# An attention kernel on one core: the first part's sums in the same steps as its scores, V and q/k jobs moved to other steps, and the low parts of the weights taken from SBUF

## What is computed

```
xf = x.reshape(b, c, n)                                # 8, 128, 1024
q = einsum('oc,bcn->bon', Wq, xf) + bq                 # 64 x 1024 for each image
k = einsum('oc,bcn->bon', Wk, xf) + bk                 # 64 x 1024
v = einsum('oc,bcn->bon', Wv, xf) + bv                 # 128 x 1024
attn = softmax(einsum('bci,bcj->bij', q, k), axis=-1)  # 1024 x 1024
out = einsum('bcn,bmn->bcm', v, attn)
return gamma * out + x
```

## Time and profile before

| | us |
|---|---|
| median of 3 runs | 240.18 |
| lowest, highest | 240.05, 241.45 |
| the profiled execution's own time | 239.82 |
| its span in the profile | 238.0 |
| TensorE busy (matmul) in the span | 221.8 (93%) |
| ScalarE busy | 177.9 (75%) |
| GpSimd busy | 177.5 (75%) |
| VectorE busy | 161.0 (68%) |

### The profile page before, as it was taken

The page is one execution under the profiler, slowest core; times in us unless marked ns, Lnnn a source line. Parts: engine busy times, 40 slices in busy tenths (PEclk is TensorE's granted clock), DMA queues, the critical chain, the costliest instruction groups (busy, mean ns, idle before and its releaser), DMA issues.

```text
span 238.0 us, 5352 instructions
## 1 busy us (share of the span) xinstructions
PE 221.8 (93%) x1864; PEld 205.0 (86%) x1864; DVE 161.0 (68%) x345; ACT 177.9 (75%) x342; POOL 177.5 (75%) x162
## 2 busy tenths in 40 slices
PE   6786958799999999999999999999999999999994
PEld 5464857599998999899998999899998999999994
DVE  1676556787776677777776677767776687676334
ACT  2486856668887798778877798778877788778980
POOL 8667665967877788778887787778886866886871
PEclk9999999999999999999999999999999999999999
DMA  3652640067700945048600964039400862100111
GB/s 95 212 211 64 156 136 1 4 144 166 223 0 3 234 120 178 2 106 208 214 10 0 218 153 164 2 89 221 139 0 0 196 159 88 49 0 3 44 48 44
DMA packets 17882, 24.43 MB, mean 103 GB/s; under 512 B 9920, under 2 KB 10688, under 8 KB 17856
## 3 DMA queue, kind: packets, MB, share of 16 engines
q1 hardware_dynamic: 17552, 23.96, 38.6%
q10 hardware_dynamic: 304, 0.13, 0.2%
HBM read 8.59 MB, written 4.19 MB: 54 GB/s over the span
## 4 chain that ended last, share of the span: by engine, by line
PE 80%; DVE 6%; ACT 4%; DMA 3%; issue 3%; POOL 2%; SPq 1%; ACTq 0%; POOLq 0%
PE sums L615 22%; PE sums L629 12%; PE scores L594 11%; PE scores L595 11%; PE work L550 10%; PE work L544 6%; ACT qk_hi L746 2%; DVE qk_lo L840 2%; DMA k_hione<-qk_hi 2%; DMA w_qk<-in_L_conv_Wk 1%; PE work L537 1%; PE work L539 1%; PE work L538 1%; PE sums L550 1%; DVE neg_max L849 1%
## 5 line engine op out<-in xcount | busy, mean ns | idle before, releaser
L476 POOL TENSOR_TENSOR weight_lo<-weight,weight_hi 128x512 bf16<-128x512 f32 x96 | 123.1, 1290 | 40.7 <-ACT weight_hi L788 40.6
L849 DVE TENSOR_REDUCE neg_max<-work 128x1 f32<-128x512 f32 x120 | 82.0, 686 | 12.2 <-PE work L550 12.2
L615 PEld LDWEIGHTS sums<-values,weight_hi 128*128 128x128 f32 x504 | 76.6, 189 | 6.7 <-issue 2.0
L615 PE MATMUL sums<-values,weight_hi 128*128 128x258 f32 x504 | 80.8, 282 | 1.7 <-DVE weight_lo L887 1.7
L788 ACT ACTIVATE weight_hi<-scores 128x512 fp32r<-128x512 f32 x128 | 76.4, 597 | 0.0
L594 PE MATMUL scores<-q_hihi,k_hilo 128*128 128x256 f32 x256 | 71.0, 300 | 0.5 <-ACT weight_hi L788 0.5
L595 PE MATMUL scores<-q_lomax,k_hione 128*128 128x256 f32 x256 | 66.2, 281 | 0.0
L785 ACT ACTIVATE weight<-scores 128x512 f32<-128x512 f32 x96 | 57.5, 599 | 10.0 <-PE scores L595 3.6
L550 PE MATMUL work<-k_hilo,q_hihi 128*128 128x512 f32 x120 | 48.4, 406 | 4.7 <-DVE qk_lo L840 3.3
L594 PEld LDWEIGHTS scores<-q_hihi,k_hilo 128*128 128x128 f32 x256 | 48.3, 189 | 2.1 <-issue 1.6
L595 PEld LDWEIGHTS scores<-q_lomax,k_hione 128*128 128x128 f32 x256 | 48.5, 189 | 1.0 <-issue 0.5
(11 more groups left out here) (85 smaller groups left out, 162.4 us busy)
## 6 DMA issues: line engine op xcount, KB each, us to landing
x_turned_sb<-in_x_turned SPq DMA_DIRECT2D x8, 512.0 KB, 4.6
out<-y_sb SPq DMA_DIRECT2D x15, 256.0 KB, 3.4
x_sb<-in_x SPq DMA_DIRECT2D x7, 512.0 KB, 4.5
q_hihi<-qk_hi SPq DMA_DIRECT2D x12, 256.0 KB, 4.4
q_lomax<-qk_lo SPq DMA_DIRECT2D x7, 256.0 KB, 5.7
k_hione<-qk_hi SPq DMA_DIRECT2D x7, 256.0 KB, 5.2
k_hilo<-qk_hi SPq DMA_DIRECT2D x6, 256.0 KB, 3.2
k_hilo<-qk_lo SPq DMA_DIRECT2D x6, 256.0 KB, 5.1
```

Of the source, the lines that this page charges most:

```text
L476: pool.tensor_tensor(weight_lo[:, r], weight[:, r], weight_hi[:, r], ALU.subtract).then_inc(weight_lo_pool_done, 1)
L615: last = pe.matmul(sums[:, u % 2 * PAIR + it, 0:VCOLS], weight_hi[:, r, part_tile(kt, it)], values[p][:, key_tile(s, kt)], start=(j == 0 a ...
L849: dve.reduce_max(neg_max[:, t, h:h + 1], place, AX.X, negate=True).then_inc(neg_max_done, 1)
```

## The change

The high sums of part 0 are made in steps 0 to 3, in the same steps as the scores two ahead, instead of two steps later; steps 4 and 5 have no high sums, and from step 6 on all is as before. The low sums of part 0 stay in step 5. For this `project_v(0, 1)` goes to the third bank of `sums`, and q and k of image 1 go to the fourth and then the third. VectorE takes the first maximum of chunk 1 ahead of the low part of V. y of part 0 is made at step 6 instead of 8.

"v" jobs for image b + 1 move from k = 11 and 15 to 3 and 15 (7 and 15 for b = 0); "qk" jobs for image b + 2 from k = 6 and 10 to 7 and 11 (10 and 13 for b = 0). The high and low parts of x, the bf16 copies of V and the adding of the bias move with them. `EARLY_MAXES` and two of the "mt" jobs change steps.

VectorE's low parts read `weight` and `weight_hi` from SBUF; ScalarE writes all exact weights to SBUF. Both waits for the shared bank go. The low part of step 2 goes to GpSimd (31 steps on VectorE, 97 on GpSimd).

```diff
 EARLY_MAXES = {0: (1, 1, 1), 1: (1, 2, 1), 2: (1, 3, 1), 3: (1, 4, 1), 4: (1, 5, 1), 5: (1, 6, 1), 6: (1, 7, 1),
-               7: (2, 0, 2), 8: (2, 2, 2), 9: (2, 4, 1), 10: (2, 5, 1), 11: (2, 6, 2),
-               12: (3, 0, 2), 13: (3, 2, 1), 14: (3, 3, 1), 15: (3, 4, 2), 16: (3, 6, 1), 17: (3, 7, 1)}
-MAX_TURNS = {0: ("mt", 0, 1), 3: ("mt", 1, 0), 7: ("mt", 1, 1)}
+               7: (2, 0, 1), 8: (2, 1, 2), 9: (2, 3, 2), 10: (2, 5, 1), 11: (2, 6, 2),
+               12: (3, 0, 1), 13: (3, 1, 1), 14: (3, 2, 2), 15: (3, 4, 1), 16: (3, 5, 2), 17: (3, 7, 1)}
+MAX_TURNS = {0: ("mt", 0, 1), 4: ("mt", 1, 0), 8: ("mt", 1, 1)}
+QK_STEPS, FIRST_QK_STEPS = (7, 11), (10, 13)
+V_STEPS, FIRST_V_STEPS = (3, 15), (7, 15)
+X_HI_STEPS, X_LO_STEPS = (4, 8), (5, 9)
...
-    if k in (6, 10) and b + 2 < BATCHES:
-        jobs.append(("qk", b + 2, (6, 10).index(k)))
-    if k in (11, 15) and b + 1 < BATCHES:
-        jobs.append(("v", b + 1, (11, 15).index(k)))
+    qk_steps, v_steps = (FIRST_QK_STEPS, FIRST_V_STEPS) if b == 0 else (QK_STEPS, V_STEPS)
+    if k in qk_steps and b + 2 < BATCHES:
+        jobs.append(("qk", b + 2, qk_steps.index(k)))
+    if k in v_steps and b + 1 < BATCHES:
+        jobs.append(("v", b + 1, v_steps.index(k)))
...
 def low_on_dve(s):
-    return s % PART_STEPS == DVE_LOW
+    return s >= PART_STEPS and s % PART_STEPS == DVE_LOW
...
 def finish_step(part):
-    return PART_STEPS * part + PART_STEPS + AHEAD + (2 if part == 0 else 0)
+    return PART_STEPS * part + PART_STEPS + AHEAD
...
-                if k in (0, 12) and s > 0 and b + k // 12 < BATCHES:
-                    short_values(b + k // 12, 1 - k // 12)
-                if s in (4, 8):
-                    add_bias((4, 8).index(s))
-                if b == 0 and k in (5, 9) or b > 0 and k in (1, 5) and b + 2 < BATCHES:
-                    rest_of_x(b + 2, (5, 9).index(k) if b == 0 else (1, 5).index(k))
-                if b == 0 and k in (10, 13) or b > 0 and k in (9, 13) and b + 1 < BATCHES:
-                    add_bias(2 * (b + 1) + k // 13)
+                if k == 0 and b > 0:
+                    short_values(b, 1)
+                if k == (10 if b == 0 else 6) and b + 1 < BATCHES:
+                    short_values(b + 1, 0)
+                if s == 4:
+                    add_bias(0)
+                if k == (8 if b == 0 else 1):
+                    add_bias(HALVES * b + 1)
+                if k in X_LO_STEPS and b + 2 < BATCHES:
+                    rest_of_x(b + 2, X_LO_STEPS.index(k))
+                if k == 13 and b + 1 < BATCHES:
+                    add_bias(HALVES * (b + 1))
...
                 if j == 0:
                     wait(pe, y_done, PAIR * (u - 1))
-                    pe.wait_ge(weight_lo_done, low_count(s + DVE_LOW))
...
-            pe.wait_ge(neg_max_done, CHUNK_TILES + 1)
-            project_v(0, 1, sums[:, 0])
+            pe.wait_ge(neg_max_done, CHUNK_TILES + PAIR + 1)
+            project_v(0, 1, sums[:, PAIR])
...
-                if LAG <= s < ALL_STEPS:
-                    if s == LAG:
-                        pe.wait_ge(first_v_rest_done, 1)
+                if s < PART_STEPS:
+                    if s == 0:
                         pe.wait_ge(neg_max_done, CHUNK_TILES + PAIR)
-                    if s == LAG + PART_STEPS:
+                    sums_hi(s)
+                elif PART_STEPS + LAG <= s < ALL_STEPS:
+                    if s == PART_STEPS + LAG:
                         pe.wait_ge(qk_lo_done, HALVES)
                     sums_hi(s - LAG)
-                    if (s - LAG) % PART_STEPS == PART_STEPS - 1:
-                        sums_lo(s - LAG)
-                if s in (1, 2):
-                    pe.wait_ge(neg_max_done, CHUNK_TILES + PAIR + s)
-                    project_qk(1, s - 1, sums[:, PAIR + s - 1])
+                if LAG <= s < ALL_STEPS and (s - LAG) % PART_STEPS == PART_STEPS - 1:
+                    sums_lo(s - LAG)
+                if s == 1:
+                    pe.wait_ge(neg_max_done, MAXES)
+                    project_qk(1, 0, sums[:, PAIR + 1])
+                if s == 2:
+                    pe.wait_ge(first_v_rest_done, 1)
+                    project_qk(1, 1, sums[:, PAIR])
...
-                if low_on_dve(s):
-                    u = s // PART_STEPS
-                    wait(act, y_done, PAIR * (u - 1))
-                    if u == 0:
-                        act.wait_ge(neg_max_done, CHUNK_TILES + PAIR)
-                    if u == 1:
-                        act.wait_ge(qk_lo_done, HALVES)
-                act.activation(exact_weights(s) if low_on_dve(s) else weight[:, r], scores[:, s % 2], ACT.Exp)
+                act.activation(weight[:, r], scores[:, s % 2], ACT.Exp)
...
-                if b == 0 and k in (4, 8) or b > 0 and k in (0, 4) and b + 2 < BATCHES:
-                    round_x(b + 2, (4, 8).index(k) if b == 0 else (0, 4).index(k))
+                if k in X_HI_STEPS and b + 2 < BATCHES:
+                    round_x(b + 2, X_HI_STEPS.index(k))
...
-                dve.tensor_tensor(weight_lo[:, r], exact_weights(s), weight_hi[:, r], ALU.subtract).then_inc(weight_lo_done, 1)
+                dve.tensor_tensor(weight_lo[:, r], weight[:, r], weight_hi[:, r], ALU.subtract).then_inc(weight_lo_done, 1)
...
-            dve.wait_ge(v_hi_done, HALVES)
-            dve.tensor_tensor(values[0][:, quarter(1), 0:CHANNELS], by_tiles(sums[:, 0]),
-                              values[0][:, quarter(1), CHANNELS:2 * CHANNELS], ALU.subtract).then_inc(first_v_rest_done, 1)
             for name, c, i in FIRST_MAXES:
                 do_max(c, i)
+            dve.wait_ge(v_hi_done, HALVES)
+            dve.tensor_tensor(values[0][:, quarter(1), 0:CHANNELS], by_tiles(sums[:, PAIR]),
+                              values[0][:, quarter(1), CHANNELS:2 * CHANNELS], ALU.subtract).then_inc(first_v_rest_done, 1)
```

More of the change, by code:

```diff
@@ L283, in part_banks @@
             return slice(u % 2 * PAIR, (u % 2 + 1) * PAIR)
-        def exact_weights(s):
-            return sums[:, s // PART_STEPS % 2 * PAIR + 1]
         def key_tile(s, kt):
@@ L817, in _ @@
             first_q(1, bank(0))
-            round_v(0, 1, sums[:, 0])
+            round_v(0, 1, sums[:, PAIR])
             exponentials(1)
@@ L825, in _ @@
                 if s in (1, 2):
-                    round_qk(1, s - 1, sums[:, PAIR + s - 1])
+                    round_qk(1, s - 1, sums[:, PAIR + 2 - s])
                 if s >= LAG and (s - LAG) % PART_STEPS == PART_STEPS - 1:
@@ L968, in _ @@
                 if s in (1, 2):
-                    rest_of_qk(1, s - 1, sums[:, PAIR + s - 1])
+                    rest_of_qk(1, s - 1, sums[:, PAIR + 2 - s])
                 if s + 1 < ALL_STEPS and low_on_dve(s + 1):
```

## The result

The changed kernel takes 233.06 us (median of 4 runs, 232.45 to 233.38) against 240.12 (4 runs, 239.71 to 241.45): a ratio of 0.969, 95% interval 0.965 to 0.974. The forecast was 233.2. The profiled execution took 232.45 us with a span of 230.7, 7.4 less than before's profiled one.

The account below looks back on a forecast made before the run. TensorE was taken to set the pace. Early gain 5.1 plus steady gain 2.3 minus 0.4 for VectorE's low parts makes 7.0 us: 239.82 to 232.8, plus 0.36 for the median, 233.2 us; range 231.0 to 236.4.

Parts of the forecast that it names:

- The early steps: Steps 0 to 17, worked out one by one from unit times: step 18 starts at 52.2 us, before 57.31.
- Steps 7 to 12: TensorE's early steps with V and q/k jobs and chunk 2's maxima: from 28.0 us to 40.5 us.
- a job's bank is free 1.7 us after its end: Sums bank of a V or q/k job: free once ScalarE and VectorE have read it, 1.7 us after the job.
- Step 1: Early step with a q/k job of image 1: maximum waits for VectorE's second reduction until 18.76, step ends 20.4 us.
- step 3: Early step on TensorE without a side job: 1.20 us long, ending at 23.7 us.
- The row of maxima: Chunk 2's row, needed by step 14's scores: last maximum 38.6, DMAs 40.05, row 44.05; step 14 gives back 0.8 us.
- The early gain, 5.1: Start to step 18: step 17 ends at 52.2 us where before it was 57.31, so 5.1 us less.
- The steady gain, 2.3: Images after the early steps: V's wait for q/k's bank goes, 0.65 - 0.2 = 0.45 us for each of five images.
- The 0.2 behind k = 11: Steady state: a maximum two steps behind the q/k job at k = 11 just misses its bank, costing about 0.2 us.
- VectorE's low parts: Both inputs in SBUF: 0.69 us alone, up to 1.97 if taking turns with GpSimd; 0.4 us cost over the run.
- 1.3 us of lateness is swallowed: Maximum behind a late low part: its bank is wanted 2.4 us later and reading takes 1.1, so 1.3 us is harmless.
- the wait in step 2: TensorE's 1.66 us idle in step 2, waiting for VectorE's low part in the shared bank: forecast to go.

Follow-up runs that it names:

- e10: Changed kernel with image 2's q/k in steps 11 and 13, chunk 2's last maximum first in step 11, chunk 3's maxima paired in 13 and 15: 231.5 us, 0.964.
- e2: Kernel before with only the steady-state places of the V, q/k and related jobs changed, images 1 and later: 237.92 us, ratio 0.991.
- e1: Changed kernel with VectorE's low parts (from part 1 on) read from the shared PSUM bank again, with its two waits: 233.01 us, ratio 0.970.
- e3: Kernel before with only VectorE's low parts, all 32, read from SBUF: 237.55 us, ratio 0.989.
- e8: Changed kernel with VectorE's low parts from PSUM again and y of part 0 back at step 8: 235.23 us, ratio 0.978.
- e5: Changed kernel with chunk 2's last maxima two in step 10 and one in step 11, instead of one and two: 232.57 us, ratio 0.967.

## Why the prediction was right

- **The early steps.** 35.7 us forecast from step 0 to 18, 36.17 and 36.13 measured. Steps 7 to 12 were given 2.0, 2.5, 2.4, 2.0, 2.4, 1.2 and took 2.00, 2.59, 2.41, 1.96, 2.54, 1.18. The rule that a job's bank is free 1.7 us after its end carried steps 8, 11 and 16. Step 1 was given too much (2.6 for 2.12) and step 3 too little (1.2 for 1.61), together 0.1 off: by the start of the next scores, part of the time of a q/k job of image 1 is seen only in the step behind it.
- **The row of maxima.** The last maximum came 22.10 us after step 0 (forecast 22.1), the DMAs 1.45 later (forecast the same). From the first issue to step 14 it took 4.53 and, in the second profile, 4.23, where I had 4.0. This is nearly the whole error of the early part. The term that was short is the landing of the fourth DMA, 2.63 us after its issue in the changed kernel and 2.33 in its second profile, where I had put 2.0. In the kernel before the four landed 2.0 to 2.1 after issue, in e10 1.9 to 2.0. So 2.0 was right for most of these DMAs; why this one came later in the changed kernel stays open.
- **The early gain, 5.1.** In absolute times it came out at 5.14 (step 18 at 52.17), but 0.48 of that is the chance start of step 0. The gain proper is 4.7.
- **The steady gain, 2.3.** Measured 2.17 and 2.23, and 2.31 by itself (e2). The 0.2 behind k = 11 is there: steps 25 and 29 take 2.28 against 2.10.
- **VectorE's low parts.** Forecast 0.69 and a cost of 0.4 over the run if the engines must take turns. They do: 0.68 to 1.47, mean 0.97, and TensorE loses 0.25 at most. The Trainium skill ("SBUF — State Buffer", section on SBUF's two separate sides) has it that such a pair exclude each other for a whole instruction; the runs agree, with 974 and 1409 ns together against 686 and 1290 once one input is in PSUM (e1), and with the ends of all 31 meetings. What decided the time was the second half of the argument, that 1.3 us of lateness is swallowed: no low part was more than 0.8 us late.
- **What was luck.** The sum of the gains, 7.0, fits the measured 6.8 to 6.9 better than its terms do: the early gain was 0.4 too high and the price of the turns 0.15 to 0.4 too high, and the two errors cancel.
- **What I had wrong.** I took the wait in step 2 for the only one of the shared bank and booked the rest of the early gain to the new order. In fact the bank held steps 2, 9 and 10 for 3.2 us together (1.89, 0.65 and 0.68 in e3). And "y of part 0 at step 6 ... gains nothing by itself" is true only beside the low parts from SBUF; with them in PSUM it is worth 1.8 (e8). Neither changed the sum, as the two remedies overlap.
- The copies of image 2 land in time, as reckoned; no rival came true. That step 14's wait hung on VectorE's order (e5, e10) I had not seen either; I took TensorE's bank for the cause, and in the changed kernel both give nearly the same moment (the rounding ends 23.53 us after step 0 there and 23.45 in e5).

## What to carry to other kernels

Work out a reordered stretch step by step with unit times from a quiet part of the same trace and one number for how long each bank is held; here this gave 18 steps to 0.5 us. Before adding up the parts of a change, ask for each wait which of them removes it: two parts that remove the same wait are worth one of them (3.45 and 4.75 made 4.7 here). And an engine that gets slower by 0.3 us in every fourth step may cost next to nothing, if what it makes is wanted only two steps later: read that slack before the price.

## What was unexpected in the hardware

With both inputs in SBUF, VectorE's 128x512 fp32 subtraction took up to 1.47 us beside GpSimd, and GpSimd's own operation up to 1.76 in place of 1.29. The wait for a turn stands in the profile as a longer duration of the one that came second, not as idle time before it. VectorE's operation that began first took 0.68 to 0.69, the same as with one input in PSUM (0.686). So GpSimd paid more often (31 times) than VectorE (16 times).

After an idle time of 2.08 us TensorE's clock was at 1.2 GHz for some 3.4 us in one profile (e2); after one of 2.41 us in another (before) it stayed at 2.4 GHz.

The time ahead of step 0 varied by 1.4 us between profiles, while the steps behind it agree within 0.1 in most of them. A difference of spans of under 1 us can't be read without taking that start off.
